# The entry of the last stage: the norm of the last batch in pieces between the first tiles, weights and two of ScalarE's steps moved

## The reference

```python
x = x + cross_attention_1(layernorm(x), ctx)          # one head
x = x + quantised_lora_ffn(layernorm(x))              # three blocks
x = x + cross_attention_2(ctx, layernorm(x))          # 16 heads of 16
x = x + bit_ffn(layernorm(x))                         # the last stage
```

```python
def bitlinear(x, norm_w, w):
    x_norm = rmsnorm(x, norm_w)          # x * rsqrt(mean(x^2) + 1e-8) * norm_w
    x_q = round(x_norm * s).clip(-128, 127) / s,  s = 127 / max|x_norm| of the row
    w_q = ternary(w)
    return x_q @ w_q.T
h = bitlinear(x, norm1_w, w1)            # 256 -> 1024
h = act_scale * square(relu(h)) + act_bias
y = bitlinear(h, norm2_w, w2)            # 1024 -> 256
```

## Time and profile before

| | us |
|---|---|
| median of 3 runs | 1227.3 (1223.79 to 1229.28) |
| profiled execution | 1225.0 |
| its span, first to last instruction | 1223.2 |
| PE busy | 1063.7 (87%) |
| DVE busy | 868.5 (71%) |
| ACT busy | 529.1 (43%) |
| POOL busy | 512.8 (42%) |

### The profile page before, as it was taken

How to read it: one execution, slowest core, us unless ns; L and a number is a source line. 1 busy time by engine, 2 the same in 40 slices (tenths; PEclk the granted TensorE clock), 3 DMA queues, 4 the chain that set the end, 5 groups by cost and what they waited for, 6 DMA issues and landing times.

```text
span 1223.2 us, 30795 instructions
## 1 busy us (share of the span) xinstructions
PE 1063.7 (87%) x9234; PEld 768.0 (63%) x9234; DVE 868.5 (71%) x2318; ACT 529.1 (43%) x953; POOL 512.8 (42%) x879
## 2 busy tenths in 40 slices
PE   6789999999999698989898669999999999756665
PEld 5567788777778466665664336676666666534444
DVE  4555656656666357576758669999999999578887
ACT  4313233222223211111113436666666666668886
POOL 1235444444444122222212034555555555566664
PEclk8779999999999899999999979999999999979998
DMA  8623222333223100000003686777777776640000
GB/s 227 160 62 94 83 84 86 94 94 94 86 81 91 31 1 1 0 0 0 0 1 69 138 173 152 161 169 163 163 161 166 163 163 142 201 133 26 26 26 31
DMA packets 121107, 116.08 MB, mean 95 GB/s; under 512 B 44868, under 2 KB 114023, under 8 KB 121063
## 3 DMA queue, kind: packets, MB, share of 16 engines
q1 hardware_dynamic: 119430, 115.20, 37.9%
q10 hardware_dynamic: 1632, 0.34, 0.1%
HBM read 79.15 MB, written 36.00 MB: 94 GB/s over the span
## 4 chain that ended last, share of the span: by engine, by line
PE 58%; DVE 20%; issue 8%; ACT 5%; SPq 4%; POOL 2%; DMA 1%; DVEq 1%; POOLq 0%; ACTq 0%
PE bank L1561 27%; PE bank L1719 6%; DVE nm L1326 5%; PE bank L1847 5%; PE bank L1833 4%; PE bank L1802 4%; PE bank L1655 3%; DVE hT L1258 2%; PE bank L1644 2%; PE bank L1925 2%; DVE yn L1247 2%; ACT v_all L1054 1%; POOL rs L731 1%; DVE v_all L1446 1%; ACT v_all L1049 1%
## 5 line engine op out<-in xcount | busy, mean ns | idle before, releaser
L1326 DVE TENSOR_REDUCE nm<-bank 112x1 f32<-112x375 f32 x512 | 252.8, 539 | 33.9 <-PE bank L1802 33.1
L985 ACT ACTIVATE pT<-bank 125x448 f32<-125x448 f32 x384 | 184.9, 543 | 87.8 <-PE bank L1833 86.3
L1802 PE MATMUL bank<-ks,qs 96*128 96x375 bf16 x512 | 163.5, 332 | 8.9 <-DVE nm L1326 7.6
L1833 PE MATMUL bank<-qs,ks 128*128 128x112 bf16 x1536 | 137.9, 214 | 5.7 <-DMA qs<-mrow 5.4
L1833 PEld LDWEIGHTS bank<-qs,ks 128*128 128x128 bf16 x1536 | 111.9, 99 | 29.5 <-issue 5.4
L1847 PE MATMUL bank<-pT,vaug 125*32 125x112 f32 x3072 | 101.1, 264 | 0.6 <-ACT pT L985 0.5
L936 ACT ACTIVATE yT<-bank,bcol,gcol 128x448 f32<-128x448 f32 x48 | 32.2, 721 | 160.3 <-PE bank L1701 160.3
L1719 PE MATMUL bank<-wffT,hT 128*112 128x256 f32 x384 | 99.0, 391 | 0.0
L1561 PE MATMUL bank<-wv1T,ctxT 128*125 128x256 f32 x384 | 88.0, 379 | 0.0
L1561 PE MATMUL bank<-ctxT,wk1T 128*128 128x375 f32 x256 | 86.3, 479 | 0.0
L917 ACT ACTIVATE pr<-bank,ebias 112x375 f32<-112x375 f32 x32 | 18.3, 573 | 156.2 <-DVE ebias L1178 156.2
(11 more groups left out here) (206 smaller groups left out, 2298.1 us busy)
## 6 DMA issues: line engine op xcount, KB each, us to landing
k_parts_dram<-kp SPq DMA_DIRECT2D x192, 93.8 KB, 3.5
ks<-k_parts_dram SPq DMA_DIRECT2D x64, 281.2 KB, 4.1
cnat<-in_ctx_dram SPq DMA_DIRECT2D x32, 375.0 KB
ks<-k_parts_dram SPq DMA_DIRECT2D x64, 187.5 KB, 4.2
ks<-k_parts_dram SPq DMA_DIRECT2D x64, 93.8 KB, 3.8
q_parts_dram<-qp SPq DMA_DIRECT2D x48, 112.0 KB, 2.2
qs<-q_parts_dram SPq DMA_DIRECT2D x64, 84.0 KB, 3.4
x_stream<-in_x_dram SPq DMA_DIRECT2D x4, 896.0 KB, 13.6
```

The costliest lines, as they stand in the source:

```text
L985: act.activation(pT[:, u % 6, :], B3[u % 3][0:TP], ACT.Exp).then_inc(probs_made, 1)
L1326: dve.tensor_reduce(nm[:, h:h + 1], scores[0:L], AX_X, ALU.max, negate=True).then_inc(head_max_taken, 1)
L1802: mm(A3[h % 2 if first else h % 3], qs[par][0:KS, h * L:h * L + P], ks[par][0:KS, h * T:(h + 1) * T], start=True, stop=True).then_inc(max_ ...
L1833: last = mm(B3[c][:, j * L:(j + 1) * L], ks[par][:, h * T + c * TP:h * T + c * TP + P], qs[par][:, h * L:(h + 1) * L], start=True, stop=True)
```

## The change

- SP: the three loads of stage 4's weights move from `moves(30)` to `moves(28)`.
- GpSimd: factors4 is cut into three functions of the same eight operations. Those of batch 31 and its norm_y, which stood ahead of stage 4, now follow block 0, 1, 2 and 3. The loop over the other tiles keeps two tiles a turn; four more blocks are written out.
- ScalarE: xq_out(1) goes ahead of relu(0); squares(0) goes ahead of block 0, so ahead of xq_out(2).
- TensorE: fin_turn(31) goes ahead of in_product(0), and in_turn(1) and in_product(1) no longer wait for x4(31); that wait now stands ahead of block 0 alone.

```diff
-                if isinstance(b, int) and b == B - 2:
+
+                if isinstance(b, int) and b == B - 4:
                     sp.wait_ge(ffn2_weights_in, 16)
                     everywhere_late(n2_bc, L1_ffn_norm2_w, HID)
                     sp.dma_start(w1T4.rearrange("p k n -> p (k n)"), wd[0]).then_inc(ffn2_weights_in, 16)
...
-            def factors4(b):
-
-
-                chained = [0]
-
+            def linked(b, done):
                 def link(ins):
-                    chained[0] += 1
+                    done[0] += 1
                     ins.then_inc(ffn2_row_factor_steps, 1)
-                    pool.wait_ge(ffn2_row_factor_steps, 10 * b + chained[0])
+                    pool.wait_ge(ffn2_row_factor_steps, 10 * b + done[0])
                     apart(pool, passed_pool)
+                return link
+
+            def variance_root(b):
+                link = linked(b, [0])
                 v, at = mv4[:, row(b), 1], row(b)
                 pool.wait_ge(ffn2_row_stats, 3 * b + 3)
                 apart(pool, passed_pool)
                 link(pool.tensor_tensor(t4[:, at], v, eps4[0:L, 0:1], ALU.add))
                 link(pool.tensor_tensor(rs4[:, at], t4[:, at], mhalf[0:L, 0:1], ALU.pow))
+
+            def mean_square(b):
+                link = linked(b, [2])
+                v, at = mv4[:, row(b), 1], row(b)
                 link(pool.tensor_tensor(t4[:, at], v, rs4[:, at], ALU.mult))
                 link(pool.tensor_tensor(t4[:, at], t4[:, at], rs4[:, at], ALU.mult))
                 link(pool.tensor_tensor(t4[:, at], t4[:, at], eps4[0:L, 1:2], ALU.add))
+
+            def scale_and_shift(b):
+                link = linked(b, [5])
+                at = row(b)
                 link(pool.tensor_tensor(rr4[:, at], t4[:, at], mhalf[0:L, 0:1], ALU.pow))
                 link(pool.tensor_tensor(rs4[:, at], rs4[:, at], rr4[:, at], ALU.mult))
                 link(pool.tensor_tensor(rr4[:, at], mv4[:, row(b), 0], rs4[:, at], ALU.mult))
...
-            for b in range(B - 3, B):
+            for b in range(B - 3, B - 1):
                 factors4(b)
                 norm_y(b)
...
             pool.wait_ge(ffn2_weights_in, 64)
-            over_tiles(pool, step4, 2, 2)
+
+            for i in range(6):
+                step4(i, i % 2, i // 2)
+                if i == 0:
+                    variance_root(B - 1)
+                if i == 1:
+                    mean_square(B - 1)
+                if i == 2:
+                    scale_and_shift(B - 1)
+                if i == 3:
+                    norm_y(B - 1)
+            with pool.Fori(0, (NT - 8) // 2) as i:
+                step4(2 * i + 6, 0, i + 3)
+                step4(2 * i + 7, 1, i + 3)
+            for i in range(NT - 2, NT):
+                step4(i, i % 2, i // 2)
...
-                if not isinstance(i, int) or i < NT:
+                if not isinstance(i, int) or 1 <= i < NT:
                     squares(i, par)
...
+            xq_out(1, 1)
             relu(0, 0)
-            xq_out(1, 1)
             square(0, 0)
+            squares(0, 0)
             over_tiles(act, step4, 4, 4)
...
             in_turn(0, 0)
+            fin_turn(B - 1)
             in_product(0, 0)
-            fin_turn(B - 1)
+            in_turn(1, 1)
             fin_project(B - 1)
+            in_product(1, 1)
             pe.wait_ge(x_after_attn2, B)
-            in_turn(1, 1)
-            in_product(1, 1)
             over_tiles(pe, step4, 4, 4)
```

More of the change, by code:

```diff
@@ L777, in factors4 @@
                 link(pool.tensor_tensor(rr4[:, at], mv4[:, row(b), 0], rs4[:, at], ALU.mult))
+            def factors4(b):
+                variance_root(b)
+                mean_square(b)
+                scale_and_shift(b)
             def norm_y(b):
```

## The result

| | before | after |
|---|---|---|
| median | 1224.88 us (1222.62 to 1229.28, 20 runs) | 1229.62 us (1226.65 to 1233.40, 20 runs) |
| ratio, 95% interval | | 1.0039 (1.003 to 1.0048) |
| span of the profiled execution | 1223.2 us | 1227.9 us |
| granted clock of TensorE, mean | 0.961 | 0.951 |

The change made the kernel slower, by 4.7 us. The forecast was 1.0 us faster (1226.3 us, range 1221 to 1230): the wrong direction. The range happens to contain 1229.62, but it was laid around a median of 1227.3 from three runs, which twenty runs put at 1224.88. Both traces carry the same difference: 1227.9 - 1223.2 = 4.7 us of span.

The account below looks back on a forecast made before the run. The last stage is paced by a TensorE-ScalarE-VectorE loop, 5.17 us a tile, entered late through GpSimd's norm. Gain -4.3 plus stall 3.3 gives -1.0 us, from a median of 1227.3 to 1226.3 us; range 1221 to 1230.

Parts of the forecast that it names:

- GpSimd's norm and the gain at round_h(0): At the last stage's entry, weigh_h(0) starts at 1066.3, not 1071.39; round_h(0) ends 4.3 us sooner (bounds 3.7 to 4.9).
- activate(0) at zero: VectorE's activate(0) at the entry comes no sooner; the projection before it moves under 0.1 us (bounds -0.1 and +0.4).
- The stall: VectorE's result(2) waits for store_out(0), issued on SP right behind load_y(3): 3.3 us lost (bounds 0 and 6.1).
- The clock: TensorE's clock: a shorter hole at the entry and new idleness near 1093 cancel, put at zero (bounds -2.8 and +2.8).
- The prediction's own sign of being wrong: Last stage: among its listed signs, blocks after 1095 running at another pace than 5.17 us would show it wrong.
- The weights at zero: SP's 1.5 MB of weights go out near 1032, not 1048.16; nothing waited for them, cost 0 (bounds -0.3 and +2).
- Rival 4: Early weights hold up ScalarE's row transfer of batch 30 before a full TensorE: up to 2 us, 1228.3; chance 0.05.
- The pieces in front of weigh_h at zero: GpSimd's mean_square and scale_and_shift ahead of weigh_h(2) and weigh_h(3) fit its waits: cost nothing, 2.4 us without that cover.
- Rival 2: VectorE's result(2) waits over 4.3 us behind SP's queue: +1.8 net (1229.1), +4.6 with the clock; chance 0.20.

Follow-up runs that it names:

- weights back: Changed kernel with the last stage's weight loads moved back to the moves of batch 30, all else as changed: 1228.99 us, ratio 1.0033.

## Why the prediction was wrong, point by point

- **GpSimd's norm and the gain at round_h(0): right, a little large.** 4.3 us predicted (bounds 3.7 to 4.9), 3.8 in the trace, of which 0.3 had been won before the entry and 0.3 by x4(31) in the new order, so 3.2 by the step itself. The mis-sized term is round_h(0) itself: I kept its 1.61 us, and it took 2.63. Its end hangs on the end of GpSimd's weigh_h(1), 0.55 us ahead of it in both kernels, and not on its own start. The prediction had weigh_h(1) over at 1073.1; with the 0.55 us that gives 1073.65 for the end of round_h(0) and not 1073.25, and it was 1073.72.
- **activate(0) at zero: right** within 0.3 us (1062.32 against 1062.94 for x4(31), half of that from before the entry).
- **The stall: right.** 3.3 us predicted, 3.43 measured; each link came as laid out (store 1.9, then 1.86; store_out(0) behind the load). That it is the cause is shown by the kernel without it (-6.2 us) and by the kernel before with it (+7.6 us).
- **The clock: this is the step that failed.** "I take the two as cancelling (bounds -2.8 and +2.8)." They did not cancel. The entry gave nothing back: its low stretch was 17 us long as before (1065.6 to 1082.6). The stall added two stretches, which cost 3.4 us in the trace, beyond the bound. I had counted one or two blocks at 1.4 us; there were three that were longer than before, since the clock falls again at 1116.8, once the loop has been set out of step. That these 3.4 us are the clock's is shown by the traces with the stall alone (3.5 us) and with the clock held up behind it (none). The prediction's own sign of being wrong had come true: the blocks after 1095 did not keep to 5.17 us. By the Trainium skill's rule (TensorE: Matmul & The Clock Gate, HAM oscillation), which I had weighed and left out of the sum, the burst behind a wait in which TensorE stood idle starts cold. The trace agrees: 3.31 us idle, and behind it eight transposes in 1.97 us. Put at +3.4 instead of 0, the sum is -1.0 + 3.4 = +2.4.
- **The weights at zero: wrong by 0.7 to 2.3 us** on the median, inside the bound of +2 or close to it. The reason given (TensorE waited for nothing, the DMA engines were idle) was true of the one execution that I read, and was no bound: a margin of 0.5 us between two issues decided, and the early weights use up part of it. Rival 4 had the mechanism with 0.05.
- **The pieces in front of weigh_h at zero: right;** the maxima did not wait for them. mean_square did hold weigh_h(2) up by some 0.5 us (it starts at 1075.76, 0.66 us behind the end of activate(2), where weigh_h(0) had followed activate(0) in 0.14), and round_h(1) took 1.50 us and not 0.99, but activate(3) is 3.8 us sooner as round_h(0) was.
- **The tail:** 1.4 us more at the end; no step of mine speaks of it. A tail as long stands in all five traces with the stall and in one of the nine without, so it goes with the stall. By what way is open: in four of the five the clock is low there for 10.2 or 10.3 us and not 6.8, in the fifth (weights back) for 6.8 as before, a little later. With it and the gain as it stood at the stall, 3.5 and not 4.3, the terms of the trace close: -3.5 + 3.4 (wait) + 3.4 (clock) + 1.4 (tail) = +4.7.
- **The reference.** Three runs gave a median of 1227.3; twenty gave 1224.88. The range was set around the first.

Rival 2 (slower by the wait on out_stored) had the right mechanism, place and sign; its price of +1.8 came from a longer stall, while the stall was as I had it and the clock made the difference, which it had only as an extra. That its +4.6 with the clock meets the measured +4.7 is luck: it is made of a stall of 6.1 us and a clock of 2.8, where 3.4 and 4.8 were measured.

## What to carry to other kernels

When work is moved later, follow the queue that its result feeds: what stood in front of other transfers with time to spare may now stand right ahead of one that somebody waits for, and a large load ahead of a small store or row transfer makes that one late even from another queue. Price a stall of the loop that sets the pace as the wait plus what the low clock takes after it: here 3.4 us of wait cost 6 to 8 us. When a VectorE operation runs beside a large one of GpSimd, look at when GpSimd's ends. And a cost put at zero because nothing waited in one trace needs its margin beside it; one of 0.5 us is no cover.

## What the runs showed of the hardware

- A DMA of 10.5 KB on ScalarE's queue, issued 0.53 us ahead of an 896 KB load on SP's, was in time; issued 0.16 us ahead of it or 0.29 us behind it, it made TensorE wait 2.69 and 2.80 us.
- VectorE's 128x1024 tensor_scalar round_h took 0.75 us alone and up to 2.63 us beside GpSimd's 128x1024 product. In all 14 traces, when it started more than 0.1 us ahead of the end of such a product, it ended 0.54 to 0.58 us after that end. The maximum over the same 128x1024 took 1.22 us beside the product in the kernel before and 1.21 us elsewhere.
- In all five traces with a stall of 3.3 to 3.7 us of the pacing loop near 1100, the last tiles, 110 us later, took some 1.4 us longer than in the kernel before.
- Matmuls put in to hold the clock gave back 1.5 to 2.1 us where 2.5 to 7 had been expected. In each of the four traces with such matmuls the clock fell at another idle place later.
